# Masked attention with split probabilities: a head's two halves side by side, turned over by one transfer

## The chip, the cores and the metric

The kernel runs on one core of a Trainium2 chip. The metric is the device time of one execution in microseconds. Five engines work at once, each through its own list of instructions: PE (TensorE, matrix products into PSUM), DVE (VectorE), ACT (ScalarE), POOL (GpSimd) and SP (SyncE, which here only waits and issues transfers). They order themselves by semaphores. Transfers run on 16 DMA engines; SP's go through queue q1, ACT's through q10.

## The reference

```python
qkv = (x @ w_qkv).reshape(b, n, 3, H, hd).transpose(2, 0, 3, 1, 4)
attn = jnp.einsum('bhnd,bhmd->bhnm', q, k) * scale
attn = jnp.where(attn_mask[None, None] == 0, -jnp.inf, attn)
attn = jax.nn.softmax(attn, axis=-1)
o = jnp.einsum('bhnm,bhmd->bhnd', attn, v).transpose(0, 2, 1, 3).reshape(b, n, d)
o = o @ w_proj + b_proj
...
return _layernorm(x + o + ln)
```

Here b = 16, n = 1024, d = 512, H = 8 heads of hd = 64, all in float32; ln is the layer norm of o with gamma and beta, and attn_mask is adj, a 1024 x 1024 matrix of zeros and ones.

## The kernel before

**Tiling.** The float32 products are made of float16 ones: a number is split into a high half and a low half (the rest), and a product is high x high + high x low + low x high. The work is cut into groups, one for each batch element and pair of heads (16 x 4 = 64), and a group into eight *units*, each one tile of 128 query rows for both heads of the pair (ab = 0 and 1). There are 512 units and 1024 heads of 128 x 1024 probabilities.

**The path of one head.** PE makes the scores (`unit_scores`, L387). DVE adds the mask and takes the row minimum of the negated scores into p32 (`take_max`, L616). ACT takes the exponential in place (`exponential`, L479). One unit later ACT writes the high half as float16 (`high_part`, L492), and POOL subtracts it from p32 for the low half (`low_part`, L722). SP then turns both halves over, so that the keys lie on the partitions: `turn`, a DMA transpose from `p_hi` or `p_lo` into `pt` (L279), 256 KB each. Three units after the scores PE multiplies with v (`times_v`, L408 to L410).

**Buffers.** p32, p_hi and p_lo are rings of RING = 4 heads, two units. pt holds TURNED = 8 heads, each with a semaphore `turned[slot]` of its own. ACT may write a head's high half when the low half of four heads earlier has landed (L490); DVE may write p32 when the low half of four heads earlier has been made (L613); SP may fill a slot of pt when PE has multiplied with the head that was in it (`pv_done`, L278).

**Order.** Each engine runs one body for each group, with 32 slots (four to a unit), and hand-made tables (ORDER, TAKE_ACT, TAKE_DVE, NORM_SLOTS) say in which slot the side work stands: the products for q, k and v, the output projection, the layer norm. DVE, ACT and POOL share the layer norm; POOL's parts of it stand between its low halves. In the last group of each batch element PE also turns over the next batch's x tiles (XT). SP has no side work: its list is, for each unit, high of head 0, high of head 1, low of head 0, low of head 1, each behind its waits. `wait_alone` puts a wait on an instruction of its own, ahead of the transfer. ACT also issues the loads and stores of x_res and the loads of x_in, four transfers of 256 KB and one of 512 KB a group.

`pt` also serves once, at the start, as the place where adj is staged (`adj_in`, L194), and `p_lo` holds one row of the bias for a while (L440, L572).

Of the kernel before, what the change touches and what calls it, by code (L numbers as in the profile page):

```python
# [17 lines left out]
UNITS = T  # L18
QUARTERS = 4
SLOTS = UNITS * QUARTERS  # L20
RING = 4
TURNED = 8
# [102 lines left out]
def wait(eng, sem, value):  # L125

    if known(value) and value <= 0:
        return
    eng.wait_ge(sem, value)


def wait_alone(eng, sem, value):

    if known(value) and value <= 0:
        return
    eng.wait_ge(sem, value)
    eng.nop(nofuse=True)


def attention_block(nc, x, adj, w_qkv, w_proj, b_proj, gamma, beta, out):  # L140
# [3 lines left out]
    with ExitStack() as ctx:  # L144
        def sb(name, shape, dt):
            return ctx.enter_context(nc.sbuf_tensor(name, shape, dt))
# [19 lines left out]
        q_hi, q_lo = sb("q_hi", [P, N], F16), sb("q_lo", [P, N], F16)  # L166
        v_both = sb("v_both", [P, T, 2, 2 * HD], F16)
        p32 = sb("p32", [P, RING, N], F32)
        p_hi = sb("p_hi", [P, RING, N], F16)
        p_lo = sb("p_lo", [P, RING, N], F16)  # L170
        pt = sb("pt", [P, 2, TURNED, T, P], F16)
        o_pair = sb("o_pair", [P, T, P], F32)
        ot = sb("ot", [P, 2, 2, KC, T, P], F16)
        row_min = sb("row_min", [P, RING], F32)
# [16 lines left out]
        staging = ot[:, :, :, :, :, :].rearrange("p a b k t n -> p (a b k t n)").bitcast(F32)  # L191
        w_in = staging[:, 0:KC * 3 * D].rearrange("p (k n) -> p k n", k=KC)
        wp_in = staging[:, KC * 3 * D:KC * 4 * D].rearrange("p (k n) -> p k n", k=KC)
        adj_in = pt[:, 0, :, :, :].rearrange("p s t n -> p (s t n)").bitcast(F32).rearrange("p (a n) -> p a n", n=N)  # L194
        ADJ_SLOTS = 4

        def pb(name, banks):
# [42 lines left out]
        def heads(g, u, ab):  # L240

            return g * (2 * UNITS) + (2 * u + ab)

        def turned_before(g, u, ab):

            return g * (32 * 2 * UNITS // TURNED) + 32 * ((2 * u + ab) // TURNED)

        def normalised(g, u):

# [6 lines left out]
        @block.sync  # L256
        def _(sp):
            for t in range(T // 2):
                sp.dma_start(x_in[:, t, :, :], x_pairs[t, :, :, :]).then_inc(x_in_loaded[t], 16)
                sp.dma_start(w_in[:, t, :], w_qkv[t * P:(t + 1) * P, :]).then_inc(w_loaded, 16)  # L260
            for t in range(ADJ_SLOTS):
                sp.dma_start(adj_in[:, t, :], adj[t * P:(t + 1) * P, :]).then_inc(adj_loaded[t], 16)
            for t in range(ADJ_SLOTS, T):
                sp.wait_ge(mask_ready, t - ADJ_SLOTS + 1)
                sp.dma_start(adj_in[:, t % ADJ_SLOTS, :], adj[t * P:(t + 1) * P, :]).then_inc(adj_loaded[t % ADJ_SLOTS], 16)
            for kc in range(KC):
                sp.dma_start(wp_in[:, kc, :], w_proj[kc * P:(kc + 1) * P, :]).then_inc(wp_loaded, 16)
            for dst, src in ((gamma_b, gamma), (beta_b, beta)):
                sp.dma_start(dst[:, :], src.rearrange("(o n) -> o n", o=1).broadcast_to([P, D])).then_inc(const_loaded, 16)
            for row in (0, BIAS_LO):  # L270
                sp.dma_start(x_res[row:row + 1, 0, :], b_proj.rearrange("(o n) -> o n", o=1)).then_inc(const_loaded, 16)
            sp.wait_ge(mask_ready, T)

            def turn(g, u, ab, half, source, done):
                head = 2 * u + ab
                wait_alone(sp, done, heads(g, u, ab) + 1)
                if half == HI:
                    wait_alone(sp, pv_done, heads(g, u, ab) - (TURNED - 1))  # L278
                sp.dma_start_transpose(pt[:, half, head % TURNED, :, :], source[:, head % RING, :]  # L279
                                       ).then_inc(turned[head % TURNED], 16)  # L280

            def body(g):
                for u in range(UNITS):
                    ug, uk = unit_before(g, u, 1)
                    running = active(ug, "A")
                    if running:
                        turn(ug, uk, 0, HI, p_hi, hi_done)
                        turn(ug, uk, 1, HI, p_hi, hi_done)
                    if running:
                        turn(ug, uk, 0, LO, p_lo, lo_done)  # L290
                        turn(ug, uk, 1, LO, p_lo, lo_done)

            bodies(sp, body)
            for i in range(2):
                sp.wait_ge(stored[i], 16 * B * T // 2)

        @block.tensor
        def _(pe):
# [92 lines left out]
            def times_v(g, u, ab):  # L391

                ug, uk = unit_before(g, u, PV_LAG)
                if not active(ug, "A"):
                    return
                slot = (2 * uk + ab) % TURNED
                wait_alone(pe, turned[slot], turned_before(ug, uk, ab) + 32)
                if ab == 0:
                    if uk % NORM_UNITS == 0:
                        wait_alone(pe, o_done, normalised(ug, uk))  # L400
                    if uk == 0:
                        wait_alone(pe, side_dve, side_done(g, "V1"))
                at = (uk % NORM_UNITS * 2 + ab) * HD
                o = pv_bank[:, at:at + HD]
                for kt in range(T):
                    hi, lo = pt[:, HI, slot, kt, :], pt[:, LO, slot, kt, :]
# [19 lines left out]
        def _(act):  # L426
# [6 lines left out]
            def prepare_projection():  # L433
                act.wait_ge(wp_loaded, 16 * KC)
                for kc in range(KC):
                    nc.scalar.activation(wp_hi[:, kc, :], wp_in[:, kc, :], ACT.Copy, scale=WSCALE).then_inc(w_hi_ready, 1)
                act.wait_ge(const_loaded, 64)
                act.wait_ge(bias_zero, 1)
                nc.scalar.activation(bias_rows[0:1, :], x_res[0:1, 0, :], ACT.Copy, scale=WSCALE).then_inc(bias_ready, 1)
                nc.scalar.activation(p_lo[BIAS_LO:BIAS_LO + 1, 0, 0:D], x_res[BIAS_LO:BIAS_LO + 1, 0, :], ACT.Copy,  # L440
                                     scale=WSCALE).then_inc(bias_ready, 1)

            def transposed(g, i):
# [38 lines left out]
            def high_part(g, u, ab):  # L482

                ug, uk = unit_before(g, u, 1)
                if not active(ug, "A"):
                    return
                head = 2 * uk + ab
                before = unit_before(ug, uk, RING // 2)
                if not known(before[0]) or before[0] >= 0:
                    wait(act, turned[(head - RING) % TURNED], turned_before(before[0], before[1], ab) + 32)  # L490
                act.wait_ge(exp_done, heads(ug, uk, ab) + 1)
                nc.scalar.activation(p_hi[:, head % RING, :], p32[:, head % RING, :], ACT.Copy).then_inc(hi_done, 1)  # L492

            def store(g, i):
                if not active(g, "P0"):
# [53 lines left out]
        def _(dve):  # L549
# [15 lines left out]
            def prepare_projection():  # L565
                for kc in range(KC):
                    dve.wait_ge(w_hi_ready, KC + kc + 1)
                    nc.vector.scalar_tensor_tensor(wp_lo[:, kc, :], wp_in[:, kc, :], WSCALE, wp_hi[:, kc, :],
                                                   ALU.mult, ALU.subtract).then_inc(w_ready, 2)
                dve.wait_ge(bias_ready, 3)  # L570
                nc.vector.scalar_tensor_tensor(bias_rows[BIAS_LO:BIAS_LO + 1, :], x_res[BIAS_LO:BIAS_LO + 1, 0, :],
                                               WSCALE, p_lo[BIAS_LO:BIAS_LO + 1, 0, 0:D], ALU.mult, ALU.subtract  # L572
                                               ).then_inc(bias_ready, 1)

            def transposed(g, i):
# [128 lines left out]
        def _(pool):  # L704
# [8 lines left out]
            def low_part(g, u, ab):  # L713

                ug, uk = unit_before(g, u, 1)
                if not active(ug, "A"):
                    return
                slot = (2 * uk + ab) % RING
                if known(ug) and ug == 0 and uk == 0 and ab == 0:
                    pool.wait_ge(bias_ready, 4)  # L720
                pool.wait_ge(hi_done, heads(ug, uk, ab) + 1)  # L721
                nc.gpsimd.tensor_tensor(p_lo[:, slot, :], p32[:, slot, :], p_hi[:, slot, :], ALU.subtract  # L722
                                        ).then_inc(lo_done, 1)

            def layer_norm(g, i, part):
# [53 lines left out]
```

## Time and profile before

| | |
|---|---|
| median of three runs | 3394.47 us (3382.21 to 3395.74) |
| the profiled execution | 3382.03 us, span 3380.2 us |
| PE busy | 3084.6 us, 91% |
| POOL busy | 2716.8 us, 80% |
| ACT busy | 2572.4 us, 76% |
| DVE busy | 2273.7 us, 67% |
| q1 (SP's transfers) | 2166372 packets, 548.15 MB, 87.0% of 16 DMA engines |
| q10 (ACT's transfers) | 54000 packets, 100.16 MB, 10.8% |
| transposes issued by SP | 1024 from p_hi, 1024 from p_lo |

Busy shares are averages over the whole program. Idle time of an engine costs only where other work waits for it, so the waits are followed from one engine to the next. SP has no busy time in the profile, since issuing does not count as work; how long each issue holds SP's queue (SPq) is seen in the order of time and in the view of its line.

### The profile page before, as it was taken

The numbers are of one execution on the slowest core, as the hardware profiler recorded it, in microseconds if no ns is written. First come the engines' busy times: TensorE is split into PE (matmuls) and PEld (weight loads), VectorE is DVE, ScalarE is ACT, GpSimd is POOL, SyncE is SP. The second block draws the span as 40 slices with busy tenths as digits, with TensorE's granted clock in tenths as the row PEclk, the third lists the DMA queues.
The fourth block names the chain that finished last, engine by engine and source line by source line (L and its number), as shares of the span: only waits on it lengthen the run. The fifth ranks groups of instructions, "written<-read, shape, count | busy, mean of one in ns | idle before, by whom it ended". The sixth has DMA issues, their size and how long they took to land.

```text
span 3380.2 us, 122707 instructions
## 1 busy us (share of the span) xinstructions
PE 3084.6 (91%) x42624; PEld 1901.9 (56%) x42624; DVE 2273.7 (67%) x4371; ACT 2572.4 (76%) x3723; POOL 2716.8 (80%) x1543
## 2 busy tenths in 40 slices
PE   6888999999999999999999999999999999999984
PEld 3555555555655556555555655556555555655552
DVE  5556676666767677676676766667676666766664
ACT  6777777777878778778787877878777787877770
POOL 3667888787888878878787987878888787987884
PEclk9999999999999999999999999999999999999997
DMA  8999999999999999999999999999999999999992
GB/s 212 179 172 182 203 190 201 185 199 194 201 203 188 204 191 199 202 188 200 190 203 189 203 204 183 204 185 202 205 193 197 190 202 191 203 204 181 203 189 66
DMA packets 2220429, 649.09 MB, mean 192 GB/s; under 512 B 2168146, under 2 KB 2168146, under 8 KB 2220372
## 3 DMA queue, kind: packets, MB, share of 16 engines
q1 hardware_dynamic: 2166372, 548.15, 87.0%
q10 hardware_dynamic: 54000, 100.16, 10.8%
q8 instruction: 38, 0.62, 0.1%
q14 instruction: 19, 0.16, 0.0%
HBM read 77.60 MB, written 33.55 MB: 33 GB/s over the span
## 4 chain that ended last, share of the span: by engine, by line
POOL 52%; issue 32%; SPq 10%; PE 2%; DMA 1%; DVE 1%; POOLq 1%; ACT 0%; ACTq 0%; DVEq 0%
POOL p_lo L722 43%; SPq L279 10%; POOL x_res L741 3%; POOL x_res L732 2%; POOL norm L738 2%; POOL norm L735 2%; PE proj L369 1%; DMA pt<-p_lo 1%; POOLq L721 0%; PE side L351 0%; DMA x_in<-in_x 0%; PE scores_a L387 0%; DMA pt<-in_adj 0%; PE side L316 0%; DVE proj L659 0%
## 5 line engine op out<-in xcount | busy, mean ns | idle before, releaser
L722 POOL TENSOR_TENSOR p_lo<-p,p_hi 128x1024 f16<-128x1024 f32 x1024 | 2170.9, 2137 | 596.7 <-ACT p_hi L492 595.7
L492 ACT ACTIVATE p_hi<-p 128x1024 f16<-128x1024 f32 x1024 | 1052.5, 1051 | 383.7 <-DMA pt<-p_lo 379.6
L479 ACT ACTIVATE p<-p,row_min 128x1024 f32<-128x1024 f32 x1024 | 1167.0, 1141 | 160.2 <-DVE row_min L616 159.0
L616 DVE CUSTOM_DVE_ANT_0 p<-scores_a,mask_q 128x1024 f32<-128x1024 f32 x512 | 626.4, 1223 | 459.1 <-PE scores_b L387 401.8
L408 PE MATMUL pv_bank<-v_both,pt 128*128 128x64 f16 x8192 | 835.1, 194 | 87.4 <-DMA pt<-p_lo 74.8
L408 PEld LDWEIGHTS pv_bank<-v_both,pt 128*128 128x128 f16 x8192 | 743.6, 99 | 218.2 <-issue 147.4
L410 PE MATMUL pv_bank<-v_both,pt 128*128 128x64 f16 x8192 | 836.0, 194 | 0.0
L409 PE MATMUL pv_bank<-v_both,pt 128*128 128x64 f16 x8192 | 835.8, 194 | 0.0
L409 PEld LDWEIGHTS pv_bank<-v_both,pt 128*128 128x128 f16 x8192 | 733.6, 99 | 73.8 <-issue 4.1
L410 PEld LDWEIGHTS pv_bank<-v_both,pt 128*128 128x128 f16 x8192 | 734.3, 99 | 0.0
L616 DVE CUSTOM_DVE_ANT_0 p<-scores_b,mask_q 128x1024 f32<-128x1024 f32 x512 | 624.2, 1219 | 4.8 <-POOL p_lo L722 1.7
L351 PE MATMUL side<-xt_hi,w_hi 128*128 128x512 f16 x1024 | 397.2, 388 | 39.4 <-DVE xt_lo L582 27.8
L351 PE MATMUL side<-xt_lo,w_hi 128*128 128x512 f16 x1024 | 396.0, 387 | 0.0
L351 PE MATMUL side<-xt_hi,w_lo 128*128 128x512 f16 x1024 | 394.1, 385 | 0.0
L387 PE MATMUL scores_a<-k_hi,q_hi 64*128 64x512 f16 x1024 | 307.9, 381 | 68.0 <-DVE row_min L616 65.6
L340 PE MATMUL side<-w_hi,xt_hi 128*128 (+1 forms) x2048 | 366.1, 219 | 1.2 <-DVE q_lo L605 1.2
L340 PE MATMUL side<-w_lo,xt_hi 128*128 (+1 forms) x2048 | 366.9, 219 | 0.0
L340 PE MATMUL side<-w_hi,xt_lo 128*128 (+1 forms) x2048 | 366.7, 219 | 0.0
L369 PE MATMUL proj<-wp_hi,ot 128*128 128x512 f16 x1024 | 335.4, 391 | 27.5 <-DVE x_res L664 27.5
L387 PE MATMUL scores_b<-k_hi,q_hi 64*128 64x512 f16 x1024 | 309.7, 383 | 0.0
L387 PE MATMUL scores_b<-k_hi,q_lo 64*128 64x512 f16 x1024 | 304.4, 377 | 0.0
L387 PE MATMUL scores_a<-k_hi,q_lo 64*128 64x512 f16 x1024 | 304.4, 377 | 0.0
(68 smaller groups left out, 5071.9 us busy)
## 6 DMA issues: line engine op xcount, KB each, us to landing
x_res<-in_x ACTq DMA_DIRECT2D x128, 256.0 KB, 3.7
out<-x_res ACTq DMA_DIRECT2D x128, 256.0 KB, 3.2
x_in<-in_x ACTq DMA_DIRECT2D x63, 512.0 KB, 4.3
pt<-p_hi SPq DMA_TRANSPOSE x1024, 3.4
pt<-p_lo SPq DMA_TRANSPOSE x1024, 3.5
pt<-in_adj SPq DMA_DIRECT2D x8, 512.0 KB, 9.5
ot<-in_L_gnn_w_qkv SPq DMA_DIRECT2D x4, 768.0 KB, 8.8
x_in<-in_x SPq DMA_DIRECT2D x4, 512.0 KB, 7.4
```

The source lines that it names most:

```text
L279: sp.dma_start_transpose(pt[:, half, head % TURNED, :, :], source[:, head % RING, :]).then_inc(turned[head % TURNED], 16)
L340: mm = nc.tensor.matmul(bank[:, c * P:(c + 1) * P], rows[:, k, t * P:(t + 1) * P], w[:, k, OF_V, pair(g), :], start=(i == 0), stop=(i % 12 ...
L351: mm = nc.tensor.matmul(bank[:, :], w[:, k, what, p, :], xt[:, k, half * CH:(half + 1) * CH], start=(i == 0), stop=(i == LENGTH[kind] - 1))
L369: mm = nc.tensor.matmul(proj[:, :], ot[:, (HI, LO, HI)[part], parity(c), k, t, :], (wp_hi, wp_hi, wp_lo)[part][:, k, :], start=(i == 0), s ...
L387: mm = nc.tensor.matmul(scores[ab][:, keys], left[rows, q], right[rows, keys], start=(n == 0), stop=(n == 2))
L408: nc.tensor.matmul(o, hi, v_hi, start=(kt == 0 and at == 0), stop=False, skip_group_check=True)
L409: nc.tensor.matmul(o, hi, v_lo, start=False, stop=False, skip_group_check=True)
L410: mm = nc.tensor.matmul(o, lo, v_hi, start=False, stop=(kt == T - 1), skip_group_check=True)
L479: nc.scalar.activation(p32[:, slot, :], p32[:, slot, :], ACT.Exp, bias=row_min[:, slot:slot + 1], scale=-1.0, accum_out=row_sum[:, head:he ...
L492: nc.scalar.activation(p_hi[:, head % RING, :], p32[:, head % RING, :], ACT.Copy).then_inc(hi_done, 1)
L616: nc.vector.tensor_tensor_reduce(out=p32[:, slot, :], in0=scores[ab][:, :], in1=mask_q[:, u, :], scale=-SCALE, scalar=3.0e38, op0=ALU.add, ...
L722: nc.gpsimd.tensor_tensor(p_lo[:, slot, :], p32[:, slot, :], p_hi[:, slot, :], ALU.subtract).then_inc(lo_done, 1)
```

## The change

The buffers `p_hi` and `p_lo` become one, `p_split`, in which the high and the low half of a head lie side by side in each partition (2 x 1024 float16). `pt` has the slot ahead of the half, so that both halves of a slot are one stretch of 4 KB in a partition. SP turns both over with one transfer of 512 KB, which waits for the low half (`lo_done`) and for the slot of pt. It waits no more for `hi_done`. A slot's semaphore now rises by 16 and no longer by 32. There are 1024 transfers in place of 2048. Everything else reads and writes the same data under new names.

```diff
-        p_hi = sb("p_hi", [P, RING, N], F16)
-        p_lo = sb("p_lo", [P, RING, N], F16)
-        pt = sb("pt", [P, 2, TURNED, T, P], F16)
+        p_split = sb("p_split", [P, RING, 2, N], F16)
+        pt = sb("pt", [P, TURNED, 2, T, P], F16)
...
-            return g * (32 * 2 * UNITS // TURNED) + 32 * ((2 * u + ab) // TURNED)
+            return g * (16 * 2 * UNITS // TURNED) + 16 * ((2 * u + ab) // TURNED)
...
-            def turn(g, u, ab, half, source, done):
+            def turn(g, u, ab):
+
                 head = 2 * u + ab
-                wait_alone(sp, done, heads(g, u, ab) + 1)
-                if half == HI:
-                    wait_alone(sp, pv_done, heads(g, u, ab) - (TURNED - 1))
-                sp.dma_start_transpose(pt[:, half, head % TURNED, :, :], source[:, head % RING, :]
+                wait_alone(sp, lo_done, heads(g, u, ab) + 1)
+                wait_alone(sp, pv_done, heads(g, u, ab) - (TURNED - 1))
+                sp.dma_start_transpose(pt[:, head % TURNED, :, :, :].rearrange("p h t n -> p (h t) n"),
+                                       p_split[:, head % RING, :, :].rearrange("p h n -> p (h n)")
                                        ).then_inc(turned[head % TURNED], 16)
...
-                    if running:
-                        turn(ug, uk, 0, HI, p_hi, hi_done)
-                        turn(ug, uk, 1, HI, p_hi, hi_done)
-                    if running:
-                        turn(ug, uk, 0, LO, p_lo, lo_done)
-                        turn(ug, uk, 1, LO, p_lo, lo_done)
+                    if active(ug, "A"):
+                        turn(ug, uk, 0)
+                        turn(ug, uk, 1)
...
-                nc.scalar.activation(p_hi[:, head % RING, :], p32[:, head % RING, :], ACT.Copy).then_inc(hi_done, 1)
+                nc.scalar.activation(p_split[:, head % RING, HI, :], p32[:, head % RING, :], ACT.Copy).then_inc(hi_done, 1)
```

SP's list in the body that loops over the groups, before, with what each instruction waits for; one unit is four transposes:

```order
L136 REGISTER_ALU [waits hi_done]
L279 DMA_TRANSPOSE pt<-p_hi 128x8x128 [waits pv_done]
L136 REGISTER_ALU
L136 REGISTER_ALU [waits hi_done]
L279 DMA_TRANSPOSE pt<-p_hi 128x8x128 [waits pv_done]
L279 DMA_TRANSPOSE pt<-p_lo 128x8x128 [waits lo_done] x2
```

The same place after the change, one unit:

```order
L136 REGISTER_ALU [waits lo_done]
L278 DMA_TRANSPOSE pt<-p_split 128x16x128 [waits pv_done]
L136 REGISTER_ALU
L136 REGISTER_ALU [waits lo_done]
L278 DMA_TRANSPOSE pt<-p_split 128x16x128 [waits pv_done]
```

The four transfers of a unit have become two, of twice the size, and the first of them now stands behind the low half of head 0; the two transfers that needed only the high halves are gone.

## Rows read from the trace of the kernel before

**Rows 1.** The page's part 5: costliest group; count | busy us, mean ns | idle before, releaser

```profile
L722 POOL TENSOR_TENSOR p_lo<-p,p_hi 128x1024 f16<-128x1024 f32 x1024 | 2170.9, 2137 | 596.7 <-ACT p_hi L492 595.7
```

**Rows 2.** The list of waits: us in total, times, longest us

```profile
ACT p_hi L492 <- DMA pt<-p_lo: 379.6, 496, 3.1
```

**Rows 3.** The view of line 279 (SP's transposes): duration ns min/median/max

```profile
L279 SPq DMA_TRANSPOSE pt<-p_hi x1024: 1231/1232/2552, 47.9 to 3295.9; - x171
L279 SPq DMA_TRANSPOSE pt<-p_lo x1024: 1231/1290/3468, 50.7 to 3301.5; - x171
...
DMA to landing us min/median/max: 3.0/3.4/7.1
```

**Rows 4.** SP in order of time: start us, us, what (x2: a pair)

```profile
1684.71 2.79 SPq L279 DMA_TRANSPOSE pt<-p_lo  x2
...
1700.06 2.68 SPq L279 DMA_TRANSPOSE pt<-p_hi  x2
1702.84 2.66 SPq L279 DMA_TRANSPOSE pt<-p_lo  x2
1705.71 2.68 SPq L279 DMA_TRANSPOSE pt<-p_hi  x2
1708.48 3.37 SPq L279 DMA_TRANSPOSE pt<-p_lo  x2
...
1720.48 3.81 SPq L279 DMA_TRANSPOSE pt<-p_lo  x2
```

**Rows 5.** The list of waits of SP's queue

```profile
SPq L137 <- ACT p_hi L492: 98.1, 31, 15.8
...
SPq L137 <- POOL p_lo L722: 27.5, 29, 1.4
```

**Rows 6.** Busy time by stretch: us, PE, PEld, DVE, ACT, POOL, PEclk, DMA, GB/s

```profile
400.00:3200.00 2800.00, 2630.54 (x36766) 1629.69 (x36765) 1944.18 (x3754) 2209.67 (x3201) 2340.76 (x1325) 0.99 0.99 196
```

**Rows 7.** DVE in order of time, its first operation of four units

```profile
1428.33 1.22 DVE L616 CUSTOM_DVE_ANT_0 p<-scores_a,mask_q 128x1024 f32<-128x1024 f32 x1
...
1443.38 1.21 DVE L616 CUSTOM_DVE_ANT_0 p<-scores_a,mask_q 128x1024 f32<-128x1024 f32 x1
...
1462.95 1.23 DVE L616 CUSTOM_DVE_ANT_0 p<-scores_a,mask_q 128x1024 f32<-128x1024 f32 x1 [1.73 <-PE scores_b L387]
...
1508.89 1.22 DVE L616 CUSTOM_DVE_ANT_0 p<-scores_a,mask_q 128x1024 f32<-128x1024 f32 x1 [1.74 <-PE scores_b L387]
```

**Rows 8.** The views of lines 506 (256 KB) and 514 (512 KB): ACT's load issues

```profile
L506 ACTq DMA_DIRECT2D x_res<-in_x x128: 341/352/410, 254.3 to 3362.0; - x128
...
L514 ACTq DMA_DIRECT2D x_in<-in_x x63: 387/411/447, 39.0 to 3188.9; - x63
```

**Rows 9.** The DMA view of 1748 to 1752: GB/s in 40 slices

```profile
GB/s 257 272 269 271 274 287 289 287 292 280 272 294 284 282 271 266 246 189 207 175 67 26 125 197 238 215 215 195 218 200 233 197 179 187 108 62 118 215 228 218
```

**Rows 10.** SP, POOL and ACT in order of time, two units

```profile
1760.49 2.69 SPq L279 DMA_TRANSPOSE pt<-p_hi  x2
...
1766.17 2.68 SPq L279 DMA_TRANSPOSE pt<-p_hi  x2
...
1756.14 4.23 POOL L722 TENSOR_TENSOR p_lo<-p,p_hi 128x1024 f16<-128x1024 f32 x2 [0.68 <-ACT p_hi L492]
1762.35 2.13 POOL L722 TENSOR_TENSOR p_lo<-p,p_hi 128x1024 f16<-128x1024 f32 x1 [1.99 <-ACT p_hi L492]
...
1767.21 2.13 POOL L722 TENSOR_TENSOR p_lo<-p,p_hi 128x1024 f16<-128x1024 f32 x1
...
1761.22 1.06 ACT L492 ACTIVATE p_hi<-p 128x1024 f16<-128x1024 f32 x1 [1.29 <-DMA pt<-p_lo]
```

**Rows 11.** SP and POOL in order of time, after the turning of x tiles

```profile
1451.26 2.68 SPq L279 DMA_TRANSPOSE pt<-p_hi  x2
1454.03 3.25 SPq L279 DMA_TRANSPOSE pt<-p_lo  x2
...
1451.21 2.14 POOL L722 TENSOR_TENSOR p_lo<-p,p_hi 128x1024 f16<-128x1024 f32 x1 [5.31 <-ACT p_hi L492]
```

More of the change, by code:

```diff
@@ L193, in attention_block @@
         wp_in = staging[:, KC * 3 * D:KC * 4 * D].rearrange("p (k n) -> p k n", k=KC)
-        adj_in = pt[:, 0, :, :, :].rearrange("p s t n -> p (s t n)").bitcast(F32).rearrange("p (a n) -> p a n", n=N)
+        adj_in = pt[:, 0:TURNED // 2, :, :, :].rearrange("p s h t n -> p (s h t n)").bitcast(F32).rearrange("p (a n) -> p a n", n=N)
         ADJ_SLOTS = 4
@@ L284, in body @@
                     ug, uk = unit_before(g, u, 1)
-                    running = active(ug, "A")
-                    if running:
-                        turn(ug, uk, 0, HI, p_hi, hi_done)
-                        turn(ug, uk, 1, HI, p_hi, hi_done)
-                    if running:
-                        turn(ug, uk, 0, LO, p_lo, lo_done)
-                        turn(ug, uk, 1, LO, p_lo, lo_done)
+                    if active(ug, "A"):
+                        turn(ug, uk, 0)
+                        turn(ug, uk, 1)
             bodies(sp, body)
@@ L396, in times_v @@
                 slot = (2 * uk + ab) % TURNED
-                wait_alone(pe, turned[slot], turned_before(ug, uk, ab) + 32)
+                wait_alone(pe, turned[slot], turned_before(ug, uk, ab) + 16)
                 if ab == 0:
@@ L405, in times_v @@
                 for kt in range(T):
-                    hi, lo = pt[:, HI, slot, kt, :], pt[:, LO, slot, kt, :]
+                    hi, lo = pt[:, slot, HI, kt, :], pt[:, slot, LO, kt, :]
                     v_hi, v_lo = v_both[:, kt, ab, 0:HD], v_both[:, kt, ab, HD:2 * HD]
@@ L439, in prepare_projection @@
                 nc.scalar.activation(bias_rows[0:1, :], x_res[0:1, 0, :], ACT.Copy, scale=WSCALE).then_inc(bias_ready, 1)
-                nc.scalar.activation(p_lo[BIAS_LO:BIAS_LO + 1, 0, 0:D], x_res[BIAS_LO:BIAS_LO + 1, 0, :], ACT.Copy,
+                nc.scalar.activation(p_split[BIAS_LO:BIAS_LO + 1, 0, LO, 0:D], x_res[BIAS_LO:BIAS_LO + 1, 0, :], ACT.Copy,
                                      scale=WSCALE).then_inc(bias_ready, 1)
@@ L489, in high_part @@
                 if not known(before[0]) or before[0] >= 0:
-                    wait(act, turned[(head - RING) % TURNED], turned_before(before[0], before[1], ab) + 32)
+                    wait(act, turned[(head - RING) % TURNED], turned_before(before[0], before[1], ab) + 16)
                 act.wait_ge(exp_done, heads(ug, uk, ab) + 1)
-                nc.scalar.activation(p_hi[:, head % RING, :], p32[:, head % RING, :], ACT.Copy).then_inc(hi_done, 1)
+                nc.scalar.activation(p_split[:, head % RING, HI, :], p32[:, head % RING, :], ACT.Copy).then_inc(hi_done, 1)
             def store(g, i):
@@ L571, in prepare_projection @@
                 nc.vector.scalar_tensor_tensor(bias_rows[BIAS_LO:BIAS_LO + 1, :], x_res[BIAS_LO:BIAS_LO + 1, 0, :],
-                                               WSCALE, p_lo[BIAS_LO:BIAS_LO + 1, 0, 0:D], ALU.mult, ALU.subtract
+                                               WSCALE, p_split[BIAS_LO:BIAS_LO + 1, 0, LO, 0:D], ALU.mult, ALU.subtract
                                                ).then_inc(bias_ready, 1)
@@ L721, in low_part @@
                 pool.wait_ge(hi_done, heads(ug, uk, ab) + 1)
-                nc.gpsimd.tensor_tensor(p_lo[:, slot, :], p32[:, slot, :], p_hi[:, slot, :], ALU.subtract
+                nc.gpsimd.tensor_tensor(p_split[:, slot, LO, :], p32[:, slot, :], p_split[:, slot, HI, :], ALU.subtract
                                         ).then_inc(lo_done, 1)
```

## The prediction

> **What bounds the kernel now.** I call a unit the two heads of one row tile (heads 0 and 1 of the unit); there are 512 of them, and four groups of eight units make a batch. The list by line says where to begin: POOL's low half is the costliest line, 2137 ns a head, and POOL is idle before it for 596.7 us, of which 595.7 us end with ACT's high half [rows 1]. Follow that idle time in the list of waits. ACT's high half in its turn waits 379.6 us, in 496 of its 1024 places, for the landing of a low half's transposing transfer [rows 2]. So POOL heads the chain that ended last, but what stands behind it is SP's transfers. The view of line 279 shows that each half head (256 KB) occupies SP for 1.232 us at the least and 1.29 us at the median of the low halves, and that it lands 3.4 us after its issue [rows 3]. Now lay these end to end: in SP's order of time a unit without disturbance begins at 1700.06 and the next at 1705.71, which is 5.65 us of almost nothing but issuing [rows 4]. Over the whole program the first issue is at 47.9 and the last high one at 3295.9 [rows 3], so the mean unit takes 3248/511 = 6.35 us. SP waits in all of that only 98.1 + 27.5 us for ACT and POOL, 0.25 us a unit [rows 5]. SP's queue is full nearly always, and the units above 5.65 are those in which a low pair's issue is stretched (3.37 and 3.81 us in place of 2.66) [rows 4].
>
> What comes next behind SP? PE is busy 2630 of 2800 us [rows 6], 94%. Its own pace can be read where SP does not hold it: after the x tiles of a new batch have been turned, the pipeline is drained and refills, and DVE's first operation of a unit, which follows PE's scores, goes from 1462.95 to 1508.89 in eight units, 5.74 us each; the turning itself puts 15.05 us between two units, 1428.33 to 1443.38 [rows 7]. A batch at PE's pace is then 31 x 5.74 + 15.05 = 193.0 us. It now takes 32 x 6.35 = 203.3 us.
>
> **The change, part by part.**
>
> *Waits and pauses of SP.* Before, each high transfer has two waits ahead of it and each low one a single wait. The pauses can be read off: 1702.74 to 1702.84 with one wait (0.10), 1705.50 to 1705.71 with two (0.21) [rows 4]. A unit has two of each, 0.62 us. After, it has two transfers with two waits each, 0.42 to 0.43 us. Saved: 0.19 us; with rounding of the inner pauses (2.68 - 2 x 1.232 = 0.22, and 2.66 - 2 x 1.29 = 0.08) I take 0.18 us a unit. On the path, since SP's queue is the one that is full.
>
> *Issue of 512 KB in one instruction.* No row has one. Upper bound: in proportion, 2 x 1.232 = 2.46 us, or 2.52 with the 0.06 that the low halves show. Lower bound: a part of each issue is fixed and is paid once. The nearest rows are ACT's plain loads, 352 ns for 256 KB and 411 ns for 512 KB [rows 8]; doubling adds 59 ns, so about 293 ns is fixed. If a transposing issue holds the same fixed part, the long one takes 2.46 - 0.29 = 2.17 us, and a unit saves another 0.59 us. Can the DMA engines follow? 256 KB in 1.232 us is 213 GB/s, and in tenths of a microsecond behind a backlog they moved up to 294 GB/s [rows 9]; 512 KB in 2.17 us asks 242. They can. I take the fixed part as saved, because the two load rows are a measurement of just that on this chip, though on another kind of transfer. The Trainium skill speaks against it: "DMA: Bandwidth & Descriptors", section "Why a DMA increments its semaphore by 16 and not by 1", gives for generations before its newest one a sequencer cost that grows in proportion to the tiles of an SBUF to SBUF transpose, with one command for each tile. No row here shows whether that leaves a fixed part; by that rule the saving would be 0.18 us a unit and not 0.77, which is the first rival below.
>
> *Order of the halves.* Before, SP runs high 0, high 1, low 0, low 1. The high ones may begin while POOL still makes the low halves. After, nothing of a head goes before its low half is made. What covers this is SP's lag: at 1760.49 SP begins a unit whose low halves were done at 1758.25 and 1760.37 (POOL's pair from 1756.14, 4.23 us), so head 0 is 2.2 us early, and head 1, wanted at about 1763.2, 2.8 us early [rows 10]. The next unit is the tight one of a group, where POOL has layer-norm work between its low halves: low 0 is done at 1764.48 for 1766.17, low 1 at 1769.34 for 1768.8, 0.5 us late [rows 10]. Against this the ring turns sooner: ACT's high half of two units on waits for the landing of head 0's low half, 2.77 + 3.4 = 6.2 us after the unit's first issue; after the change head 0 is issued first and lands at 2.46 + 2.2 = 4.7 us (2.2 being 3.4 - 1.23). ACT waited 1.29 us just there [rows 10]. That gives POOL 1.5 us back in the half of the places where the ring holds it, for head 0; head 1 stays where it was, at 7.3 in place of 7.5. I cost the order at 0.3 us for the tight unit, 64 x 0.3 = 20 us.
>
> *After the x tiles.* Here there is no lag. SP begins a high pair at 1451.26, with POOL's low half from 1451.21 to 1453.35 beside it, and is done with the unit at 1457.28 [rows 11]. After, head 0 begins at 1453.35 + 0.1, head 1 at about 1456.1, and the unit ends at 1458.5: 1.2 us later. Some 15 batches: 18 us, if nothing takes it up. PE multiplies with these probabilities three units later, so it is at the end of the range rather than in the middle; I count it in full.
>
> *PE, DVE, ACT and POOL* run the same instructions on the same sizes; the bias row that lies for a while in the low half's buffer and the staging of adj in pt move with them, once each, at no cost. PE takes head 0's probabilities first, and they land earlier, which can only help.
>
> *The sum.* SP needs 0.18 + 0.59 = 0.77 us less a unit, 6.35 to 5.58 with its present stretches and waits, which is under PE's 5.74. So PE becomes the bound, and a batch takes 193.0 in place of 203.3 us: 16 x 10.3 = 165 us. The profiled execution took 3382.0 us (span 3380.2), so 3382 - 165 + 20 + 18 = 3255 us. The median of the runs shown, 3394.5, is 12 us above that execution, which is the lowest of them; I add the same: about **3265 us**, 3.8% faster.
>
> **The rivals.**
>
> 1. *The issue grows in proportion, and SP stays the bound.* For it: all 2048 issues have the same floor of 1.231 us [rows 3], as a loop over pieces would, and the page named above says so. Against it: the load rows. Then only the pauses are saved: 512 x 0.18 = 92 us, less 18 after the x tiles: 3382 - 92 + 18 + 12 = 3320 us.
>
> 2. *POOL takes SP's place.* SP now depends on POOL for every transfer. If POOL's timing does not follow, each step that SP gains turns into a wait for the low half, first in the tight unit where it is already 0.5 us late, then back through the group. POOL's work is 84% of the time (2340.8 of 2800 us [rows 6]), 5.3 us of 6.35, so it has room, but it comes in lumps. Priced at the whole gain of rival 1: 3394 us, no change. It decides where the idle time of SP before the low half grows from 27.5 us to over 90 us.
>
> 3. *The long issue is stretched.* SP's issue is stretched where one transfer follows directly upon another: the seven low pairs from 1684.71 to 1720.48, of which four stand here, take 3.04 us on the mean, 2.95 without the inner pause, the high pairs 2.7 [rows 4]. Part of it is ACT's loads, part may be the queue that is full. If each long transfer behaves like a low pair, a unit needs 2 x 2.95 + 0.43 = 6.33 us of SP in place of 2.70 + 3.04 + 0.31 = 6.05: 512 x 0.28 = 143 us more, 3382 + 143 + 12 = 3537 us. It is slower than before from a mean issue of (6.05 - 0.43)/2 = 2.81 us on. Against it: the engines' room [rows 9], and that the stretches are rare behind an undisturbed high pair (2.66 behind 2.68 [rows 4]).
>
> **How the numbers follow.** Forecast (fixed part saved, PE the bound) 0.43; rival 1 0.28; rival 2 0.16; rival 3 0.13, with any time between 3411 and 3537. PE alone, with nothing lost, would give 3382 - 165 = 3217, and some of the 12 us may not come: the low end is 3210. The high end must take in rival 1 and its neighbourhood up to where rival 2 begins: 3375. Left out are most of rival 2, rival 3 and a little below: some 2 in 10, with half of rival 2 between 3320 and 3375. What a measurement of this kernel can tell from no change is about 0.5%, 17 us. Faster by more: the forecast, rival 1 and a little of rival 2, 0.72. Within: most of rival 2, 0.13. Slower: 0.15.
>
> **What would show it.** In the profile after: the shortest issue of the long transfer, 2.17 (forecast) against 2.46 to 2.52 us (rival 1) and a mean over 2.81 (rival 3); landing at 4.4 to 4.7 us; SP's two pauses a unit at 0.21 us; ACT's wait for the transfer well below 379.6 us in the forecast, since SP is no longer the slowest; the eight units of a group at 46 us in the forecast, 49 in rival 1; SP's wait for POOL's low half under 90 us in all, or far above it in rival 2. The forecast is wrong if the long issue saves nothing, or if PE's pace of 5.74 us, read from one refill of eight units, is not one that it can keep.

## The result and the profile after

| | before | after |
|---|---|---|
| median | 3388.34 us (4 runs, 3379.42 to 3395.74) | 3241.22 us (4 runs, 3239.09 to 3242.9) |
| ratio | | 0.9561, 95% interval 0.9541 to 0.9581 |
| span of the profiled execution | 3380.2 us | 3237.3 us |

The kernel became 4.4% faster, 147 us; 3265 us was forecast, in a range of 3210 to 3375 us.

The page after the change, parts 1, 3, 5 and 6. The queue moves the same bytes; PE is busy 94% of the span, from 91%:

```profile
PE 3056.4 (94%) x42624; PEld 1909.3 (59%) x42624; DVE 2265.5 (70%) x4371; ACT 2553.9 (79%) x3723; POOL 2719.2 (84%) x1543
...
q1 hardware_dynamic: 2133604, 548.02, 91.7%
q10 hardware_dynamic: 54000, 100.16, 9.6%
...
L718 POOL TENSOR_TENSOR p_split<-p,p_split 128x1024 f16<-128x1024 f32 x1024 | 2172.0, 2139 | 453.6 <-ACT p_split L488 451.7
...
pt<-p_split SPq DMA_TRANSPOSE x1024, 4.8
```

The stretch from 400 to 3000 us, in the columns of [rows 6]:

```profile
400.00:3000.00 2600.00, 2526.30 (x35535) 1584.96 (x35531) 1875.20 (x3632) 2125.11 (x3101) 2265.96 (x1282) 0.99 1.03 204
```

The DMA engines' share was 0.99 already before [rows 6] and is 1.03 now, with the same bytes in less time. A share over 1 means that packets are counted side by side, so this share alone does not say whether the engines set the pace; the rate does change, from 196 to 204 GB/s.

The view of line 278, SP's transposes (ns, min/median/max), which answers to [rows 3]; then the list of waits, for [rows 2], and that of SP's queue, for [rows 5]:

```profile
L278 SPq DMA_TRANSPOSE pt<-p_split x1024: 1446/2263/4717, 52.3 to 3158.5; - x171
...
DMA to landing us min/median/max: 4.2/4.8/8.9
```

```profile
ACT p_split L488 <- DMA pt<-p_split: 212.3, 269, 2.6
...
PE pv_bank L404 <- DMA pt<-p_split: 19.7, 19, 4.1
```

```profile
SPq L137 <- POOL p_split L718: 339.8, 186, 19.6
```

Before, ACT waited for a landing in 496 places and 379.6 us, and SP waited for ACT and POOL 125.6 us in all [rows 2, 5]. Now ACT waits in 269 places and 212.3 us, and SP waits 339.8 us for low halves. SP has become an engine that has time to wait.

Who sets the pace is seen on DVE in order of time, the first operation of some units, as in [rows 7]:

```profile
1370.55 1.23 DVE L612 CUSTOM_DVE_ANT_0 p<-scores_a,mask_q 128x1024 f32<-128x1024 f32 x1
...
1384.61 1.21 DVE L612 CUSTOM_DVE_ANT_0 p<-scores_a,mask_q 128x1024 f32<-128x1024 f32 x1
...
1404.16 1.22 DVE L612 CUSTOM_DVE_ANT_0 p<-scores_a,mask_q 128x1024 f32<-128x1024 f32 x1 [1.72 <-PE scores_b L383]
...
1450.09 1.23 DVE L612 CUSTOM_DVE_ANT_0 p<-scores_a,mask_q 128x1024 f32<-128x1024 f32 x1 [1.74 <-PE scores_b L383]
```

From 1370.55 to 1384.61 there are 14.06 us between two units where the x tiles are turned (15.05 before). From 1404.16 to 1450.09 are eight units, 5.74 us each, as [rows 7] had it for one refill. Measured in the same way, a group of eight units without x tiles takes 45.9 to 46.4 us in the middle of the program. Before, the first of a batch's three such groups took 46 to 47 us and the other two 49 to 50 us. A batch takes about 194.5 us; the forecast put it at 193.0, and the old length at 203.3.

### The profile page after: what moved, and what is told of

The parts are those of the page before. It is cut to its first block, busy times and chain, and to the rows that moved or that the text cites. A ratio compares the mean times of both kernels' runs of the same rounds, so it can differ in the third digit from the quotient of the medians.

```text
span 3237.3 us, 120659 instructions
## 1 busy us (share of the span) xinstructions
PE 3056.4 (94%) x42624; PEld 1909.3 (59%) x42624; DVE 2265.5 (70%) x4371; ACT 2553.9 (79%) x3723; POOL 2719.2 (84%) x1543
## 4 chain that ended last, share of the span: by engine, by line
POOL 60%; issue 29%; PE 3%; SPq 2%; DMA 2%; DVE 1%; ACT 1%; POOLq 1%; ACTq 0%; DVEq 0%
POOL p_split L718 49%; POOL x_res L737 4%; POOL x_res L728 4%; SPq L278 2%; POOL norm L734 2%; POOL norm L731 2%; DMA pt<-p_split 2%; PE proj L365 1%; PE side L347 1%; PE scores_a L383 1%; POOLq L717 0%; ACT p L475 0%; PE side L336 0%; ACT p_split L488 0%; DMA x_in<-in_x 0%
## 5 line engine op out<-in xcount | busy, mean ns | idle before, releaser
L718 POOL TENSOR_TENSOR p_split<-p,p_split 128x1024 f16<-128x1024 f32 x1024 | 2172.0, 2139 | 453.6 <-ACT p_split L488 451.7
L488 ACT ACTIVATE p_split<-p 128x1024 f16<-128x1024 f32 x1024 | 1052.2, 1048 | 215.3 <-DMA pt<-p_split 212.3
L404 PE MATMUL pv_bank<-v_both,pt 128*128 128x64 f16 x8192 | 834.1, 194 | 21.7 <-DMA pt<-p_split 19.7
L383 PE MATMUL scores_b<-k_lo,q_hi 64*128 64x512 f16 x1024 | 304.4, 377 | 0.0
```

The lines of the kernel that those rows point to most:

```text
L383: mm = nc.tensor.matmul(scores[ab][:, keys], left[rows, q], right[rows, keys], start=(n == 0), stop=(n == 2))
L488: nc.scalar.activation(p_split[:, head % RING, HI, :], p32[:, head % RING, :], ACT.Copy).then_inc(hi_done, 1)
L718: nc.gpsimd.tensor_tensor(p_split[:, slot, LO, :], p32[:, slot, :], p_split[:, slot, HI, :], ALU.subtract).then_inc(lo_done, 1)
```

## The experiments

Each kernel was timed beside the kernel before on the same chip; ratios are to that kernel. The changed kernel was not timed again beside the experiments, so it is compared with them by these ratios; its own is 0.9561. The **theory** after the result: SP's instruction costs about 1.15 us whatever it moves, and very little for the size, so that 2048 of them set the pace before; 1024 of twice the size leave SP free, and PE sets the pace. The **rivals**: the gain comes from the order (a head is complete sooner, and the ring turns sooner); from the place in memory; or from the DMA engines, which might lose time at each transfer's ends.

### Size alone, order alone, place alone

*Size alone.* The old buffers and the old order, but a transfer takes the same half of both heads:

```diff
+                wait_alone(sp, done, heads(g, u, 1) + 1)
...
+                sp.dma_start_transpose(pt[:, half, at:at + 2, :, :].rearrange("p s t n -> p (s t) n"),
+                                       source[:, slot:slot + 2, :].rearrange("p s n -> p (s n)")
+                                       ).then_inc(turned[at // 2], 16)
...
```

> The kernel before with its separate buffers and its order high, low, but one 512 KB transfer turns the same half of both heads of a unit (1024 transfers; high pair, then low pair). Same result. Theory A (SP's instruction has a fixed part of about 1 us, which 2048 issues pay and 1024 pay half as often; the minimum went from 1.231 us for 256 KB to 1.446 us for 512 KB): near the changed kernel, 3240 to 3290 us, the excess being that head 0's low half lands only with head 1's; shortest issue 1.45 us. Rival C (the gain comes from the order, since a head is complete earlier and the ring turns sooner): 3388 us, no gain.

Measured: 3308.74 us, ratio 0.9804 (0.9788 to 0.9821). Neither number: a gain of 2.0%, less than half. The views of the two high and low issues, then the waits of this kernel:

```profile
L279 SPq DMA_TRANSPOSE pt<-p_hi x512: 1684/2282/5036, 51.7 to 3215.9; - x171
L279 SPq DMA_TRANSPOSE pt<-p_lo x512: 1443/2361/4779, 55.1 to 3220.3; - x171
```

```profile
ACT p_hi L489 <- DMA pt<-p_lo: 325.0, 340, 3.3
```

```profile
SPq L137 <- POOL p_lo L719: 325.5, 241, 3.3
SPq L137 <- ACT p_hi L489: 164.9, 41, 18.2
```

The issue is as short as in the changed kernel, so this part of SP's cost is gone. What took its place, as the waits read, is a circle: a pair waits for its second head, lands for both at once, and ACT waits 325.0 us for it where it waits 212.3 in the changed kernel.

*Order alone.* The old buffers and 256 KB transfers, in the changed order and with its waits:

```diff
+                wait_alone(sp, lo_done, heads(g, u, ab) + 1)
+                wait_alone(sp, pv_done, heads(g, u, ab) - (TURNED - 1))
+                for half, source in ((HI, p_hi), (LO, p_lo)):
+                    sp.dma_start_transpose(pt[:, half, head % TURNED, :, :], source[:, head % RING, :]
+                                           ).then_inc(turned[head % TURNED], 16)
...
```

> The kernel before with its separate buffers and 256 KB transfers, but in the order and with the waits of the changed one: for each head one wait for the low half, one for pt, then high and low transfer back to back (2048 transfers). Same result. Theory A: only the pauses between transfers are saved, 512 x 0.18 = 92 us, so 3290 to 3390 us, shortest issue 1.231 us. Rival B (the DMA engines bound it by bytes and packets): 3388 us. Rival C (order): 3241 us.

Measured: 3375.73 us, ratio 1.0002 (0.9985 to 1.0019). The order by itself brings nothing. So size without the right order brings 2.0%, the order without the size nothing, both together 4.4%: they work together. This run also says what the pauses are worth. SP in order of time, two heads (start us, us):

```profile
1710.09 1.24 SPq L279 DMA_TRANSPOSE pt<-p_hi  x1
1711.37 1.33 SPq L279 DMA_TRANSPOSE pt<-p_lo  x1
1712.92 1.23 SPq L279 DMA_TRANSPOSE pt<-p_hi  x1
1714.20 1.32 SPq L279 DMA_TRANSPOSE pt<-p_lo  x1
1715.78 1.24 SPq L279 DMA_TRANSPOSE pt<-p_hi  x1
```

```profile
L279 SPq DMA_TRANSPOSE pt<-p_lo x1024: 1296/1328/4202, 54.2 to 3291.4; - x171
```

The second transfer of a head has no wait and follows after some 0.05 us, but its issue is never under 1.296 us. Two heads take 5.69 us (1710.09 to 1715.78), as a unit does in [rows 4]. Counted over all transfers from 1000 to 3000 us, the pauses of a unit, without the longer waits, fell from 0.70 to 0.59 us, and its issues grew from 5.35 to 5.42 us. So this kernel saves only a part of the pauses, and most of that comes back as longer issues.

*Place alone.* The changed buffers, with the four 256 KB transfers of before:

```diff
+                sp.dma_start_transpose(pt[:, head % TURNED, half, :, :], p_split[:, head % RING, half, :]
+                                       ).then_inc(turned[head % TURNED], 16)
...
```

> The changed kernel's buffers (halves side by side in p_split, slot ahead of half in pt), but the four 256 KB transfers of a unit in the order and with the waits of before. Same result. Both theories: no difference from the kernel before, 3378 us within 0.5%. If placement in memory mattered, it would show here.

Measured: 3389.44 us, ratio 1.0006 (0.9987 to 1.0024). The place in memory does nothing.

### What an issue costs

*Half the size.* The kernel before with transfers of 128 KB; keys 512 to 1023 are not turned, and PE reads the first four tiles twice:

```diff
-                sp.dma_start_transpose(pt[:, half, head % TURNED, :, :], source[:, head % RING, :]
+                sp.dma_start_transpose(pt[:, half, head % TURNED, 0:T // 2, :], source[:, head % RING, 0:N // 2]
...
-                    hi, lo = pt[:, HI, slot, kt, :], pt[:, LO, slot, kt, :]
+                    hi, lo = pt[:, HI, slot, kt % 4, :], pt[:, LO, slot, kt % 4, :]
```

> The kernel before with 2048 transfers of 128 KB (the first 512 keys of each half; PE reads these four tiles twice, so its work is the same and the output is another). What it measures is SP's issue. Theory A (fixed part of about 1 us and 0.215 us for 256 KB, from 1.231 and 1.446 us): shortest issue 1.1 to 1.2 us, so SP needs 4 x 1.27 = 5.1 us a unit and PE bounds: 3210 to 3250 us. Rival: the floor of 1.231 us is in proportion to the size: shortest issue 0.62 us; the time is then bounded by PE too, 3210 to 3250 us.

Measured: 3230.82 us, ratio 0.9528 (0.9502 to 0.9554). The view of its transposes:

```profile
L279 SPq DMA_TRANSPOSE pt<-p_hi x1024: 1188/1189/2458, 49.4 to 3148.4; - x171
L279 SPq DMA_TRANSPOSE pt<-p_lo x1024: 1188/1217/2495, 52.1 to 3151.4; - x171
```

128 KB cost SP 1.188 us, 256 KB 1.231 us: 43 ns more for twice the size, so some 1.145 us of each is fixed. But this kernel, with as many instructions as before, is as fast as the changed one. So the instructions alone do not set the old pace either. Four issues of 1.19 to 1.22 us and 0.62 us of pauses [rows 4] are about 5.5 us a unit, under PE's 5.74; before, the four with their pauses are 5.65 us undisturbed [rows 4], just under PE's pace too, and 6.35 us on the mean. What must be added is what lengthens them.

*The same bytes in twice as many transfers as before.* The changed kernel, each 512 KB cut into four:

```diff
+                for half in (HI, LO):
+                    for part in range(2):
+                        sp.dma_start_transpose(pt[:, head % TURNED, half, 4 * part:4 * part + 4, :],
+                                               p_split[:, head % RING, half, part * CH:(part + 1) * CH]
+                                               ).then_inc(turned[head % TURNED], 16)
...
```

> The changed kernel with each head's 512 KB cut into four transfers of 128 KB (4096 in all), issued one behind the other after the same two waits. Same result, same bytes. Theory: SP's instruction costs about 1.15 us and little for its size (1.188 us for 128 KB, 1.231 us for 256 KB), so a unit needs 8 x (1.19 to 1.25 + 0.06) + 0.4 = 10.4 to 10.9 us and the program 512 times that and 130 us, 5450 to 5700 us. Rival (bytes and the DMA engines' pace decide; each transfer's ends cost them 0.13 us): 2048 transfers more than the kernel before, 266 us over 3380: 3650 us.

Measured: 5709.58 us (two executions), ratio 1.6864 (1.677 to 1.6959). The view of its line, its q1 row, and its busy time by stretch with the DMA engines' share next to last:

```profile
L280 SPq DMA_TRANSPOSE pt<-p_split x4096: 1188/1260/2962, 50.0 to 5629.6; - x196
```

```profile
q1 hardware_dynamic: 2231908, 548.41, 48.1%
```

```profile
1000.00:4000.00 3000.00, 2049.42 (x23020) 1153.14 (x23016) 1222.66 (x2346) 1384.97 (x2005) 1472.89 (x829) 0.86 0.54 115
```

This is the clearest run of the study. The DMA engines are half idle, PE is at two thirds, SP waits for nobody (17.8 us in one place at the start), and the time is the number of instructions times their cost: (5629.6 - 50.0)/4096 = 1.362 us from issue to issue, of which 1.26 us is the issue itself. Bytes and the ends of transfers at the engines would have given 3650 us. That rules them out as the bound of this kernel; whether a transfer's ends cost the engines something in the kernel before is taken up below.

*Twice the size once more.* The changed kernel with one transfer of 1 MB a unit:

```diff
+                wait_alone(sp, lo_done, heads(g, u, 1) + 1)
...
+                sp.dma_start_transpose(pt[:, at:at + 2, :, :, :].rearrange("p s h t n -> p (s h t) n"),
+                                       p_split[:, slot:slot + 2, :, :].rearrange("p s h n -> p (s h n)")
+                                       ).then_inc(turned[at // 2], 16)
...
```

> The changed kernel with one transfer of 1 MB for both heads of a unit (512 transfers), issued when both low halves are made. Same result. By the cost of a transfer's ends (0.1 to 0.15 us of the DMA engines' time for each transfer) it saves 50 to 75 us if nothing else mattered. Against it, head 0 waits for head 1 at both ends, as in the kernel with pairs of heads, which stood 67 us over the changed kernel. I expect 3270 to 3330 us, issue at the median 4.6 to 5.0 us (DMA engines' pace of 2.50 us for 512 KB).

Measured: 3877.96 us, ratio 1.1435 (1.1402 to 1.1468), far outside what I expected. Its issue, its landing (page, part 6), and three waits:

```profile
L277 SPq DMA_TRANSPOSE pt<-p_split x512: 4672/4952/7658, 51.7 to 3792.2; - x171
```

```profile
pt<-p_split SPq DMA_TRANSPOSE x512, 6.9
```

```profile
POOL p_split L716 <- ACT p_split L486: 1089.7, 398, 45.9
ACT p_split L486 <- DMA pt<-p_split: 720.0, 247, 7.2
...
PE pv_bank L402 <- DMA pt<-p_split: 424.9, 175, 10.0
```

```profile
SPq L137 <- POOL p_split L716: 986.1, 278, 19.8
```

The issue is as I expected; its consequence is not. SP waits for POOL, POOL for ACT, ACT for the landing: a closed circle through the ring of two units. One turn is a landing (6.9 us), the first high half (1.05 us) and two low halves (4.2 us), 12.2 us at least for two units, and the layer norm's work on POOL falls into it; measured are (3792.2 - 51.7)/511 x 2 = 14.6 us. I had priced the circle with the size experiment's loss and left out that the landing time had grown from 4.8 to 6.9 us and that both heads now lie in one link of the chain. That the circle is the cause is read from the waits; a kernel with a deeper ring was not tried.

The engines' rate in this kernel while one issue of 1 MB runs, and in the kernel before, each from 1700 to 1704 us (GB/s in 40 slices of 0.1 us, above them the engines' share in tenths):

```profile
DMA  9999999999999999999999999999994000000000
GB/s 218 212 220 223 210 220 218 218 218 218 218 223 212 215 223 220 218 218 218 220 215 218 215 223 215 215 212 166 210 228 90 0 0 0 0 0 0 0 0 0
```

```profile
DMA  9999999999942899999999989626999999999996
GB/s 287 260 284 292 297 289 292 287 276 248 243 80 46 184 228 220 215 220 195 215 205 207 218 149 167 121 44 136 218 223 223 215 202 205 228 210 192 184 190 113
```

Inside the long transfer the engines keep about 218 GB/s, which is 1.2 us for 256 KB. The issue takes as long as they do: in the 199 places where the engines had stood idle for over 0.5 us ahead of it, it was still never under 4.78 us. In the kernel before, the rate falls to about 45 GB/s in these slices, once in each transfer of 256 KB, and over the stretch from 1000 to 3000 us 0.8 us a unit of the engines' time stands unused, 0.2 us for each transfer. I read this as the engines being done before SP brings the next one.

### What lengthens the old stream

*ACT's loads small, before.* In the 58 looped groups the loads of x_in and x_res move 16 of 512 columns; instructions and semaphores stay:

```diff
+                part = slice(0, D if known(g) else 16)
-                act.dma_start(x_res[:, i, :], x_tiles[projected(g, i), :, :]).then_inc(x_res_loaded[i], 16)
+                act.dma_start(x_res[:, i, part], x_tiles[projected(g, i), :, part]).then_inc(x_res_loaded[i], 16)
...
```

> The kernel before, but in the 58 groups of the loop ACT's loads of x_in and x_res move only the first 16 columns (the same instructions and semaphores, 1 MB of 1.5 MB a group less on q10; the output is another). Theory: the stream of 256 KB transfers needs 5.55 us a unit by itself and is lengthened by 0.78 us a unit by ACT's transfers (0.13 us for each 16 packets of 2 KB), because SP issues at the engines' pace and can't run ahead. Then two thirds of 0.78 us go, 0.52 x 8 x 58 = 241 us at most, stopped by PE at about 3217 to 3231 us: 3220 to 3260 us. Rival (SP's instructions and pauses alone set the pace): no gain, 3385 us.

Measured: 3286.6 us, ratio 0.9722 (0.9701 to 0.9742). Some 95 us of the old time is ACT's loads pushing into SP's stream. The expected range lay lower and was missed: it took for granted that the stream would fall under PE's pace everywhere. In the loop a batch takes 194.7 to 197.8 us here, about 197 in the median, 0.19 us a unit less than before where up to 0.52 had been put, and still some 2.4 us above the 194.6 of the changed kernel: its third group without x tiles takes 47 to 48 us. That rest is left to SP's own instructions.

*The same in the changed kernel.*

> The changed kernel with the same small loads. If PE bounds it except for what ACT's transfers still cost: 3217 to 3230 us. If the transfers' stream bounds it: well under, since PE would not.

Measured: 3239.06 us, ratio 0.9578 (0.9562 to 0.9594), where the changed kernel has 0.9561. The same loads cost the changed kernel nothing. That is the second half of the explanation: with 512 KB transfers SP may run ahead of the engines (its shortest issue is 1.446 us, while the issue of 1 MB, which the engines hold back, was never under 4.672 us, 2.34 us for 512 KB), so a delay by ACT's packets is made up. With 256 KB the instruction costs 1.231 us and a pause, the engines need about 4.672/4 = 1.17 us, so SP has nothing in hand, and what is lost once stays lost. How far SP can be ahead was not measured, so this is read from the durations and not shown by itself.

What a transfer's ends cost the engines can be bounded here. Where SP issues 512 KB transfers back to back and no transfer of ACT is in flight, they follow each other after 2.41 us in the median (378 places), against 2.34 us by the rate of 1 MB. By this estimate the ends take under 0.1 us each, so they can be a part of the 0.2 us in each transfer of the kernel before, but not all of it.

### What bounds now

*Less work for PE.* One of the three products of the probabilities with v is left out, in both kernels:

```diff
-                    nc.tensor.matmul(o, hi, v_lo, start=False, stop=False, skip_group_check=True)
```

> The kernel before without the product high x low of the probabilities with v (one of three, 8192 matmuls of 29 ns from start to start, 0.46 us a unit); the output lacks that term. If SP's queue bounds it, as I said: 3350 to 3388 us, only the time after the x tiles can gain. If PE bounds it already: 3388 - 238 = 3150 us.

> The changed kernel without the same product, 0.46 us of PE a unit less. If PE bounds it (5.74 us a unit between the turnings of x tiles): down to 3005 us if nothing else came next; with mean issues of 2.47 us and pauses SP needs 5.5 us a unit, so 3020 to 3110 us. If SP, the DMA engines or POOL still bound it: within 1% of 3241 us.

Measured: before 3353.93 us, ratio 0.9935 (0.9918 to 0.9951); after 3175.64 us, ratio 0.9416 (0.9395 to 0.9436). The old kernel hardly notices that PE has 0.46 us a unit less to do (24 us of 238), which bears out that PE did not bound it. The changed one gains 49 us by the ratios, 66 us by the two medians. PE is its bound for most of this, but another stands close behind; I expected 3110 us or less. In that kernel ACT's wait for the landing is longer again:

```profile
ACT p_split L487 <- DMA pt<-p_split: 279.0, 329, 2.6
```

and POOL is busy 2318.94 of 2600 us. The DMA engines are a third candidate: from 400 to 3000 us their share is 1.04 at 209 GB/s, the highest rate of all kernels here. Which of the three comes first, the ring, POOL or the engines, was not separated.

*Less for the DMA engines.* The changed kernel turns the high half only (1024 transfers of 256 KB), PE reads it in both places:

```diff
-                sp.dma_start_transpose(pt[:, head % TURNED, :, :, :].rearrange("p h t n -> p (h t) n"),
-                                       p_split[:, head % RING, :, :].rearrange("p h n -> p (h n)")
+                sp.dma_start_transpose(pt[:, head % TURNED, HI, :, :],
+                                       p_split[:, head % RING, HI, :]
...
-                    hi, lo = pt[:, slot, HI, kt, :], pt[:, slot, LO, kt, :]
+                    hi, lo = pt[:, slot, HI, kt, :], pt[:, slot, HI, kt, :]
```

> The changed kernel, but only the high half of each head is turned (1024 transfers of 256 KB, still issued when the low half is made) and PE reads it in both places; PE's work is the same, the output is another. It halves the load on the DMA engines. If PE alone bounds the changed kernel: no gain beyond 3217 us (193.0 us a batch). If the DMA engines' pace (2 x 2.50 us and 0.78 us for ACT's transfers, 5.78 us a unit) bounds it as well: 3217 us or a little under, with SP's waits for POOL grown. Shortest issue 1.231 us.

Measured: 3217.27 us, ratio 0.949 (0.9464 to 0.9517). With half the bytes and half the old number of instructions the time ends at what PE's pace alone gave in the prediction, 3217 us. That the two numbers are equal is partly luck, since a batch takes 194.7 us here and not 193.0. In the middle of the program this kernel, the one with 128 KB transfers and the changed one have the same pace, 194.5 to 194.7 us a batch: with the result unchanged, PE's pace is reached. The changed kernel is 24 us above this one, and 17 us of that have come about by unit 64, in the first two batches.

*The x tiles spread.* PE's, ACT's and DVE's slots for the turning of x tiles pulled apart in the changed kernel:

```diff
-XT_ACT = [14, 16, 16, 16]
-XT_DVE = [14, 16, 16, 16]
+XT_ACT = [14, 16, 17, 18]
+XT_DVE = [14, 17, 18, 19]
...
+    slots[17], slots[18], slots[19] = [("XT", 2)], [("XT", 3)] + late[:6], late[6:]
```

> The changed kernel with the turning of the next batch's x tiles spread: PE's XT items in slots 15, 16, 17, 18 in place of 15, 16, 16, 16 (the second q product squeezed into slots 18 and 19), ACT's parts in 14, 16, 17, 18 and DVE's in 14, 17, 18, 19, behind the row minima of their unit. Same result. If PE bounds the changed kernel, what is left besides its pace is the 8 us that it stands in the 15 groups with x tiles; DVE's minimum of the unit no longer waits for six tiles. 3150 to 3235 us if part of that is covered, 3241 us or more if PE's wait for ACT and DVE, tile by tile, stays as it is.

Measured: 3263.67 us, ratio 0.9648 (0.9632 to 0.9665), 0.7 to 0.9% slower than the changed kernel (by the medians and by the ratios). Groups without x tiles became longer, 46.5 in place of 46.0 us, perhaps since the second q product is squeezed there too, and those with x tiles did not become shorter (56.0 to 57.3 us; the changed kernel has mostly 56.2 to 56.9). No version here beats the changed kernel with the same result.

## Why the prediction was right

- **What bounded the kernel: right, in a narrower sense.** SP's queue was full and PE was not the bound (PE's relief brought 24 us of 238). But "SP's queue is full" had two parts that I did not separate: the instruction's own cost, and ACT's loads, which push an issue out and are never made up. Half the bytes at the same count reach PE's pace, 3231 us. Smaller loads alone do not quite, 3287 us: they bring about two thirds of the gain.
- **The pauses, 0.18 us a unit: right in size, but not shown to be worth anything.** In the changed kernel the short pauses fell from 0.70 to 0.51 us a unit. The order experiment saves 0.11 us of them, which should have brought 56 us, and gains nothing; 0.07 us comes back as longer issues. Rival 1 rested on the pauses alone, and this speaks against its 92 us, though no run saves the full 0.18 us at 256 KB.
- **The fixed part of an issue: right in kind, sized too small.** I took 0.29 us from ACT's plain loads [rows 8]. It is about 1.145 us, from 1.188 and 1.231 us for 128 and 256 KB. The nearest rows were of another kind of instruction.
- **The engines can follow 512 KB in 2.17 us: wrong.** I took the short burst of [rows 9] for a pace. The median issue is 2.263 us, the engines' pace under 1 MB transfers 2.34 us and more for 512 KB. These two errors lie against each other, so 2.17 us came near the 2.263 us seen, for the wrong reason: SP's own need is 1.446 us or less, and the engines hold it back to 2.26. On the mean the long issue takes 2.47 us, as much as rival 1 had put as its floor. So a unit's issues fell only from 5.35 to 4.88 us (1000 to 3000 us), 0.47 where 0.59 was forecast. This was enough because the stream now takes up ACT's traffic and stays under PE's 5.74 us.
- **PE as the next bound, 193.0 us a batch: right**, 194.5 us measured; 16 x (203.3 - 194.5) = 141 us of the 147. It was read from one refill of eight units, and it holds for the whole program. The 1.5 us missing in the forecast's batch are the unit behind the turning of the x tiles, which takes 7.7 us in the mean and not 5.74, less the turning itself, 14.4 us in the mean where 15.05 had been read.
- **The order of the halves, 20 us, and the start after the x tiles, 18 us: too dear.** SP does wait more for POOL, 339.8 us, but nothing behind it is late: PE waits 19.7 us for probabilities in all. These waits have taken the place of an issue, not of work. By the forecast's own sign, over 90 us of such waits, rival 2 should have come about. The sign was a bad one: an engine that no longer sets the pace waits more, whatever the reason.
- **The Trainium skill's rule.** "DMA: Bandwidth & Descriptors", section "Why a DMA increments its semaphore by 16 and not by 1", gives 262,144 cycles for 8,192 tiles of this kind of transpose, with one push command for each tile; that the cost is in proportion to the size was my reading of it. The runs differ: 43 ns more from 128 to 256 KB, 0.215 us from 256 to 512 KB. The measurement decides: up to 512 KB the cost here is almost all per instruction.
- **The chances.** The forecast had 0.43 and came about; rival 1 had 0.28 on two grounds, the common floor of all issues and the page's rule, and neither held: the floor of 512 KB is 1.446 us and not 2.46.
- **The point forecast**, 3265 us, is 24 us high: 38 us for the two items above that cost nothing and some 10 of the 12 us added for the median, against 141 us saved where 165 had been put. The terms err in both directions, so the number is nearer than its parts.

## What to carry to other kernels

Where one queue issues a stream of transposing transfers and is seldom waiting, compare the issue's shortest time at two sizes before anything else; if it hardly changes, fewer and larger transfers are worth trying. Here they also let the queue run ahead of the engines, so that the other queue's traffic no longer cost time. Stop at the size where the next link of the ring still gets its buffer in time: twice the size gave 4.4%, four times took 14%. A merge must keep the order in which consumers need the parts, or half the gain is lost in a new circle of waits.

## What was not expected of the hardware

The issue of a transposing transfer from SBUF to SBUF holds SP's queue for 1.188 us at 128 KB, 1.231 at 256 KB, 1.446 at 512 KB, each at the least, and 4.672 us at 1 MB, where the issue lasts as long as the engines move data, even if they stood idle before it. An issue that follows another directly is longer: 1.296 us at the least in place of 1.231 for 256 KB, and 1.26 us in the median in place of 1.188 for 128 KB. So of the 0.11 us of pauses that the order experiment took out of a unit, 0.07 came back in the issues.
